# A vision tower on one core: the first logits moved ahead of the later embeddings, and the last results on another engine

## The reference, cut to what matters

```python
def reference(x, tok_W, tok_b, w1, b1, ww, bw, w2, b2, gamma, beta, w_gate, w_up, w_down):
    h = patchify(x) @ tok_W.T + tok_b                # 16 images x 64 patches, 768 -> 256
    v = h @ w1.T + b1
    w = softmax((v @ ww.T + bw).reshape(..., 16, 31))  # 16 heads, 31 taps; the axis of
    c = causal_conv(v, w)                            # time holds the 16 images
    a = layer_norm(h + (c @ w2.T + b2), gamma, beta)
    h = layernorm(h + a)
    g = silu(bitlinear(h, w_gate)) * bitlinear(h, w_up)
    return layernorm(h + bitlinear(g, w_down))
# bitlinear: the activations are rounded to 255 levels by each token's largest
# magnitude, the weights to -1, 0, 1 by the mean magnitude of the whole matrix
```

## Time and profile before

| | |
|---|---|
| median of 3 executions | 122.58 us |
| lowest, highest | 120.61, 123.64 us |
| the profiled execution: its own time | 121.21 us |
| its span in the profile | 119.4 us |
| busy in the span: PE, PEld | 102.3 (86%), 66.3 (55%) us |
| busy: DVE, ACT, POOL | 75.6 (63%), 71.6 (60%), 75.2 (63%) us |
| mean granted clock of TensorE | 0.976 |
| HBM read, written | 9.43, 2.34 MB |

### The profile page before, as it was taken

The page is one execution under the profiler, slowest core; times in us unless marked ns, Lnnn a source line. Parts: engine busy times, 40 slices in busy tenths (PEclk is TensorE's granted clock), DMA queues, the critical chain, the costliest instruction groups (busy, mean ns, idle before and its releaser), DMA issues. The chain is left out here.

```text
span 119.4 us, 2363 instructions
## 1 busy us (share of the span) xinstructions
PE 102.3 (86%) x714; PEld 66.3 (55%) x714; DVE 75.6 (63%) x184; ACT 71.6 (60%) x131; POOL 75.2 (63%) x147
## 2 busy tenths in 40 slices
PE   6938997399999999999999999999999997775400
PEld 2536885377677557755755666565665653354200
DVE  5229800004464574848798989889887889978710
ACT  0006121596686330477676798998688899879620
POOL 6995000000209596999656886888888988988840
PEclk9999999999999999999999999999999999999955
DMA  3999999910122132323233220232301010010232
GB/s 100 272 384 430 422 420 381 415 68 0 49 20 24 46 33 59 38 50 34 57 34 65 22 22 0 52 32 58 34 9 32 20 28 15 0 49 0 56 90 79
DMA packets 22099, 11.94 MB, mean 100 GB/s; under 512 B 17987, under 2 KB 20291, under 8 KB 21702
## 3 DMA queue, kind: packets, MB, share of 16 engines
q1 hardware_dynamic: 21436, 10.67, 31.7%
q10 hardware_dynamic: 650, 1.11, 2.6%
HBM read 9.43 MB, written 2.34 MB: 99 GB/s over the span
## 5 line engine op out<-in xcount | busy, mean ns | idle before, releaser
L1078 POOL TENSOR_TENSOR taps<-probs,inv_total 128x256 f32<-128x256 f32 x8 | 5.1, 635 | 20.4 <-DVE inv_total L792 20.1
L351 PE MATMUL bank<-xT,first 128*128 128x256 f32 x72 | 16.4, 380 | 0.3 <-ACT h1T L583 0.3
L429 PE MATMUL bank<-conv_w,vpad 128*32 128x128 f32 x256 | 15.9, 399 | 0.0
L771 DVE TENSOR_REDUCE top<-bank 128x16 f32<-128x496 f32 x8 | 5.3, 664 | 16.4 <-PE bank L412 16.3
L351 PEld LDWEIGHTS bank<-xT,first 128*128 128x128 f32 x72 | 13.5, 190 | 3.2 <-issue 0.9
L412 PE MATMUL bank<-ww,vT 128*128 128x496 f32 x32 | 14.6, 578 | 0.0
L667 ACT ACTIVATE gu<-bank,sc 128x512 f32<-128x512 f32 x16 | 11.0, 687 | 3.7 <-PE bank L486 3.2
L854 DVE TENSOR_TENSOR gu<-gu,bank 128x512 f32<-128x512 f32 x16 | 10.9, 683 | 2.6 <-ACT gu L667 2.6
L429 PEld LDWEIGHTS bank<-conv_w,vpad 128*32 128x32 f32 x256 | 8.6, 122 | 6.4 <-issue 3.1
L1104 POOL TENSOR_SCALAR q<-gu,sc 128x512 f16<-128x512 f32 x14 | 9.7, 694 | 2.6 <-DVE sc L871 1.5
L542 PE MATMUL bank<-w_q,q2T 128*128 128x256 f16 x64 | 9.0, 272 | 2.6 <-ACT q2T L681 2.2
(11 more groups left out here) (115 smaller groups left out, 228.4 us busy)
## 6 DMA issues: line engine op xcount, KB each, us to landing
xT<-in_xT SPq DMA_DIRECT2D x3, 768.0 KB, 14.9
first<-in_first SPq DMA_DIRECT2D x2, 512.0 KB, 6.5
w_raw<-in_wg SPq DMA_DIRECT2D x1, 1024.0 KB, 11.6
w_raw<-in_wu SPq DMA_DIRECT2D x1, 1024.0 KB, 13.8
w_raw<-in_wd SPq DMA_DIRECT2D x1, 1024.0 KB, 17.6
shear<-taps SPq DMA_DIRECT2D x8, 128.0 KB, 1.7
conv_w<-shear SPq DMA_DIRECT2D x64, 16.0 KB, 2.0
out_dram<-res SPq DMA_DIRECT2D x7, 128.0 KB
```

The lines of the kernel that those rows point to most:

```text
L351: last = nc.tensor.matmul(ps_embed(pair, m), tokW[:, k, m * P:(m + 1) * P], xT[:, pair - 1, k, :], start=(k == 0), stop=(k == KC_PATCH - 1))
L429: last = nc.tensor.matmul(ps_yT[j * SLOT:(j + 1) * SLOT, k, :], vpad[:, s, h, :], conv_w[:, s, :, h], start=(par == 0), stop=(par == 1))
```

## The change

The lists of TensorE and ScalarE are written anew for the first stage. On TensorE `logits(0)` comes ahead of `embed(1, 1)`, `logits(1)` ahead of `values_turned(1, 0)` and `embed(2, 0)`, `logits(2)` ahead of `embed(2, 1)` and `logits(3)` ahead of `embed(3, 0)`. On ScalarE `weight_sum(0)`, `(1)` and `(2)` are set apart, with copies and exponentials between them; `negate_gamma()` moves behind `weight_sum(2)`, and `weight_round(1)` behind `exps(3)`. In ScalarE's last tile `out_q1T(7)` comes ahead of `scaled_down(4)` and `silus(7, 1)` ahead of `out_q2T(5)`, and `result(3)` behind `out_q2T_last()`. The results of tiles 5, 6 and 7 are made by VectorE, `late_result(t)`, all behind `out_variance(7)`; GpSimd's `shift_result(5)` and `(6)` go; `f` has four buffers. SyncE stores tile 5 and the first half of tile 7, ScalarE tile 6 and the second half of tile 7.

```diff
+LATE = 5
-        f = sb("f", [P, 3, D])
+        f = sb("f", [P, 4, D])
-        last_ok = sem("last_ok")
+        late_ok = sem("late_ok")
+        def store_late(eng, t):
+            eng.wait_ge(late_ok, t - LATE + 1)
+            eng.dma_start(out_d[:, t * BLOCK:(t + 1) * BLOCK, :].rearrange("i b d -> b i d"),
+                          res[:, t % 4, :]).then_inc(out_done[t % 4], 16)
         def store_half(eng, j):
-            eng.wait_ge(last_ok, 1)
+            eng.wait_ge(late_ok, TILES - LATE)
# SyncE
-            store(0); store(1); store(2); store(3); store(4); store(5); store(6); store_half(sp, 0)
+            store(0); store(1); store(2); store(3); store(4); store_late(sp, 5); store_half(sp, 0)
# TensorE
-            first_embeds(); embed(1, 0); embed(1, 1); values_turned(0, 0); residual(0); values_turned(0, 1)
-            values_turned(1, 0); values(0); embed(2, 0); logits(0); embed(2, 1); logits(1); values_turned(1, 1)
-            values_turned(2, 0); values(1); values_turned(2, 1); weight_means(0, 2); logits(2); embed(3, 0)
-            weight_means(2, 3); logits(3); conv(0); logits(4); project_out(0); embed(3, 1); values(2); conv(1)
+            first_embeds(); embed(1, 0); values_turned(0, 0); values_turned(0, 1); residual(0); logits(0)
+            embed(1, 1); values(0); logits(1); values_turned(1, 0); embed(2, 0); values(1); values_turned(1, 1)
+            logits(2); weight_means(0, 2); embed(2, 1); values_turned(2, 0); logits(3); values_turned(2, 1)
+            weight_means(2, 3); embed(3, 0); conv(0); logits(4); project_out(0); embed(3, 1); values(2); conv(1)
# ScalarE
-            out_h1T(0, 0); out_h1T(0, 1); out_h1T(1, 0); out_h1T(1, 1); out_vT(0, 0); negate_gamma(); out_h1(0)
-            out_vT(0, 1); out_v(0); weight_sum(0); out_vT(1, 0); weight_sum(1); out_h1T(2, 0); exps(0)
-            weight_sum(2); out_h1T(2, 1); out_vT(1, 1); exps(1); out_v(1); out_vT(2, 0); out_vT(2, 1)
-            weight_round(1); out_h1T(3, 0); exps(2); exps(3); out_yT(0); out_v(2); exps(4); out_h1T(3, 1)
+            out_h1T(0, 0); out_h1T(0, 1); out_h1T(1, 0); out_vT(0, 0); out_vT(0, 1); out_h1(0); weight_sum(0)
+            exps(0); out_h1T(1, 1); out_v(0); weight_sum(1); out_vT(1, 0); exps(1); out_h1T(2, 0); out_v(1)
+            out_vT(1, 1); weight_sum(2); out_h1T(2, 1); negate_gamma(); exps(2); out_vT(2, 0); out_vT(2, 1)
+            exps(3); weight_round(1); out_h1T(3, 0); out_yT(0); out_v(2); exps(4); out_h1T(3, 1)
...
-            quant_in(7); scaled_down(4); out_q1T(7); result(2); silus(7, 0); out_q2T(5); silus(7, 1)
-            down_scale(5); down_scale(6); scaled_down(5); out_q2T(6); quant_last_half(); result(3)
-            scaled_down(6); out_q2T_last(); result(4); result(5); result(6)
-            store_half(act, 1)
+            quant_in(7); out_q1T(7); scaled_down(4); result(2); silus(7, 0); silus(7, 1); out_q2T(5)
+            down_scale(5); down_scale(6); scaled_down(5); out_q2T(6); quant_last_half()
+            scaled_down(6); out_q2T_last(); result(3); result(4)
+            store_late(act, 6); store_half(act, 1)
# scaled_down on ScalarE; down_result on VectorE waits likewise
-                if t >= 3:
-                    act.wait_ge(res_ok, t - 2)
+                if t >= 4:
+                    act.wait_ge(res_ok, t - 3)
# VectorE
-            def last_result():
-                dve.wait_ge(rstd_out, TILES)
-                dve.wait_ge(out_done[LAST % 4], 16)
-                nc.vector.tensor_scalar(res[:, LAST % 4, :], f[:, LAST % 3, :], mv[:, 2, LAST % 4, 0:1],
-                                        rstd[:, 2, LAST % 4, 0:1], ALU.subtract, ALU.mult).then_inc(last_ok, 1)
+            def late_result(t):
+                dve.wait_ge(rstd_out, t + 1)
+                dve.wait_ge(out_done[t % 4], 16)
+                nc.vector.tensor_scalar(res[:, t % 4, :], f[:, t % 4, :], mv[:, 2, t % 4, 0:1],
+                                        rstd[:, 2, t % 4, 0:1], ALU.subtract, ALU.mult).then_inc(late_ok, 1)
-            out_stats(7); out_variance(7); last_result()
+            out_stats(7); out_variance(7); late_result(5); late_result(6); late_result(7)
# GpSimd
-            inv_std_out(4); shift_result(4); add_centred(6); inv_std_out(5); shift_result(5); inv_std_out(6)
-            shift_result(6); inv_std_out(7)
+            inv_std_out(4); shift_result(4); add_centred(6); inv_std_out(5); inv_std_out(6)
+            inv_std_out(7)
```

More of the change, by code:

```diff
@@ L696, in result @@
                     act.wait_ge(out_done[t % 4], 16)
-                nc.scalar.activation(res[:, t % 4, :], f[:, t % 3, :], ACT.Identity, bias=shift_out[:, t % 4:t % 4 + 1],
+                nc.scalar.activation(res[:, t % 4, :], f[:, t % 4, :], ACT.Identity, bias=shift_out[:, t % 4:t % 4 + 1],
                                      scale=rstd[:, 2, t % 4, 0:1]).then_inc(res_ok, 1)
@@ L715, in scaled_down @@
                 act.wait_ge(down_scale_ok, t + 1)
-                if t >= 3:
-                    act.wait_ge(res_ok, t - 2)
-                nc.scalar.activation(f[:, t % 3, :], ps_down, ACT.Identity,
+                if t >= 4:
+                    act.wait_ge(res_ok, t - 3)
+                nc.scalar.activation(f[:, t % 4, :], ps_down, ACT.Identity,
                                      scale=sc[:, t % 4, 9:10]).then_inc(down_read, 1)
@@ L923, in down_result @@
                 dve.wait_ge(centred_ok, t + 1)
-                dve.wait_ge(res_ok, t - 2)
-                nc.vector.scalar_tensor_tensor(f[:, t % 3, :], ps_down, sc[:, t % 4, 9:10], centred[:, t % 6, :],
+                dve.wait_ge(res_ok, t - 3)
+                nc.vector.scalar_tensor_tensor(f[:, t % 4, :], ps_down, sc[:, t % 4, 9:10], centred[:, t % 6, :],
                                                ALU.mult, ALU.add).then_inc(down_read, 1)
@@ L933, in out_stats @@
                     dve.wait_ge(down_read, t + 1)
-                at["out", t] = mark(nc.vector.bn_stats(stats[:, 2, t % 2, :], f[:, t % 3, :]))
+                at["out", t] = mark(nc.vector.bn_stats(stats[:, 2, t % 2, :], f[:, t % 4, :]))
             def out_variance(t):
@@ L1110, in add_centred @@
                 pool.wait_ge(centred_ok, t + 1)
-                nc.gpsimd.tensor_tensor(f[:, t % 3, :], f[:, t % 3, :], centred[:, t % 6, :], ALU.add).then_inc(f_ok, 1)
+                nc.gpsimd.tensor_tensor(f[:, t % 4, :], f[:, t % 4, :], centred[:, t % 6, :], ALU.add).then_inc(f_ok, 1)
             def weight_round(j):
```

## The result

The changed kernel takes 123.82 us (median of 4, 123.48 to 124.51) where the kernel before, with its further run, takes 121.73 (median of 4). The ratio is 1.0237, with a 95% interval of 1.0179 to 1.0295: slower, while the interval leaves open whether by more or less than 2%. All ratios here leave out executions more than 1.5% above the fastest of their kernel, which takes out two of the four of the kernel before and makes this one larger than the ratio of the medians (1.017). The profiled executions are 121.21 and 123.48 us, 2.27 apart, their spans 119.4 and 121.6.

What follows compares the result with a forecast made beforehand. TensorE's queue from conv(0) to 97 us, then the end's chain to GpSimd, was taken as the bound. First stage +1.44 and end +0.26 gave +1.70, so 122.9 or 124.3 us by footing; 123.6 was taken, range 121.0 to 125.5.

Steps and rivals of the forecast that it cites:

- The six holes: First stage, TensorE: six open hand-offs sum to 4.30 us against one hole of 2.86, so conv(0) starts 1.44 later.
- the rigid shift: From conv(0) to 97 us: TensorE is full, so any shift of conv(0)'s start arrives at 97 us undiminished.
- the cover of weight_round(1): ScalarE, behind exps(3): the 2.10 us instruction delays out_yT(0) at no cost, with 0.9 us of cover before project_out(0).
- the weight chain: First stage: the first two weight means come earlier, but weight_means(2,3) at 39.4 as before, so nothing is gained.
- The silu order: End, ScalarE: silus(7,1) ahead of out_q2T(5) wins the silu 0.57 but makes down(5) and down(7) about 1.0 us later.
- the other edits: End: taking two shifts off GpSimd saves 0.65 us, and scaled_down(6) no longer behind result(3) another 0.1.
- the queue of GpSimd: End: without two shifts ahead, GpSimd takes up the last statistics as they come, saving 0.65 us.
- VectorE's results "hidden" in GpSimd's 0.93: End: VectorE makes results 5 and 6, 0.41 us each, within the 0.93 that GpSimd needs, at no cost.
- result(3) is done ahead of down_result(7): End: the moved result(3) finishes at 112.9, before down_result(7), which waits for it, at 113.2; cost 0.
- At this kernel's density a hole did not cost the clock: First stage: the granted clock was 1.00 behind the 2.86 us hole, taken as evidence against a clock loss.
- rival C: Early stage: the clock falls and one embed costs its 2.6 us again; +4.3, time 126.9, chance 0.05.
- The middle course between two footings: Whole time: 123.6 us, taken between 122.9 on the profiled execution and 124.3 on the median of three runs.

Runs made afterwards that it cites:

- e11: The changed kernel with weight_round(1) directly behind weight_sum(2) on ScalarE; 123.08 us, ratio 1.0274 to the kernel before.
- e4: The changed kernel with out_q2T(5) ahead of silus(7,1) again; 122.99 us, ratio 1.0118 to the kernel before.
- e1: The kernel before with only the new first-stage order on TensorE and ScalarE; 123.01 us, ratio 1.0157 to the kernel before.
- e6: The changed kernel with result(3) ahead of scaled_down(6) again; 123.21 us, ratio 1.0176 to the kernel before.
- e2: The changed kernel with the old first-stage order, all edits of the end kept; 122.92 us, ratio 1.0086 to the kernel before.
- e3: The kernel before with only negate_gamma() moved, behind out_h1T(2,1) on ScalarE; 118.73 us, ratio 0.9779 to the kernel before.
- e9: The changed kernel with the gamma and beta load issued late, by SyncE behind the last xT load; 123.31 us, ratio 1.0266 to the kernel before.
- e12: The changed kernel with logits(3) behind values_turned(2,1) and out_q2T(5) ahead of silus(7,1); 121.85 us, ratio 1.0101 to the kernel before.
- e7: The changed kernel with logits(3) behind values_turned(2,1) on TensorE; 124.71 us, ratio 1.0245 to the kernel before.
- e8: The kernel before with the gamma and beta load issued late, by SyncE behind the last xT load; 127.47 us, ratio 1.0612 to the kernel before.
- e5: The changed kernel with old first-stage order, negate_gamma() behind out_h1T(2,1), out_q2T(5) before silus(7,1), result(3) before scaled_down(6); 118.68 us, ratio 0.9830 to the kernel before.

## Why the prediction was right, and where it was not

**The early part.** Right in mechanism and place. The six holes, by the same starts as in the prediction, measure 0.60, 0.83, 0.68, 0.85, 0.84 and 0.68 (the second, for one: 22.57 - 21.49 - 0.25), 4.48 against 4.30 forecast. The term was +1.44 and F grew by 1.77. The holes were undersized by 0.18 in sum. Most of that is one restart: values_turned(1,1) starts 0.26 behind the end of ScalarE's copy (28.09 + 0.47 to 28.82) and not 0.14, where the other five restarts take 0.10 to 0.15. The rest is that a group which had waited reaches its copy 0.07 later (2.87 and 1.14 in place of 2.80 and 1.07). The remaining 0.15 of F is work that the prediction held to be the same, above all embed(3,0), which takes 2.76 to conv(0) where an embed took 2.59 to the next. I had taken the price of a restart from one row, of values(0).

**The stage behind it.** Right: full TensorE from conv(0) on, the rigid shift, the cover of weight_round(1) (e11), the weight chain where it was (VectorE reads the second mean at 39.99, before at 39.73).

**The end.** +0.26 was forecast, G shows +0.64. The silu order was right: priced at 1.01, it measures 1.09 at down(5) and 1.05 in G (e4). The gain that was set against it was too large: the other edits were priced at -0.75 and gain 0.41 (e4 against e1). Step by step, from e1 to the changed kernel: down(5) +1.09; from there to the last variance -0.13, priced -0.1; the queue of GpSimd -0.54, priced -0.65, as GpSimd still starts 0.10 behind the variance (115.75 + 0.18 = 115.93 to 116.03); and from there to the last result +0.22, priced at nothing. Together 0.64.

That last step is what failed: VectorE's results "hidden" in GpSimd's 0.93, and "result(3) is done ahead of down_result(7): 0". In e6, where no store is in the way, it is 1.01 from GpSimd's start to the last result, and GpSimd's first instruction of that root takes 0.34 in place of 0.27 while two results of VectorE run; it is 0.34 in all nine profiles with an edited end and 0.26 or 0.27 in the five with the old one:

```profile
115.23 0.34 POOL L1074 TENSOR_SCALAR veps<-veps,mv 128x1 f32<-128x1 f32 x1
```

The Trainium skill (SBUF — State Buffer, in its table of terms) has the two engines arbitrate for one pair of ports, the loser blocked while the other's instruction holds it. The longer row has the direction of that, but it is longer by 0.07 only, where one result of VectorE takes 0.41, and no run here isolates it. The other 0.15 is the store of tile 3 (e6). The step on result(3) looked at one reader only: the last result also waits for that store, which the move had put back.

On E alone the end would look as forecast, +0.29 from e1 to the changed kernel. That is luck: gate(7,1) came 0.35 earlier behind conv(0) in the one profile than in the other (63.17 and 63.52).

**The clock.** "At this kernel's density a hole did not cost the clock" is the sentence that fell. The row was right and the reading too wide: one profile had the clock at 1.00 behind the hole, that of e2 at 0.74. In the 55 executions of the kernel before beside the experiments, the 23 with a mean clock of 0.976 or more have a median of 120.72 us, the 32 below it one of 122.44. Of the kernels without the open hole, the changed one, e1, e3 to e6, e9, e11 and e12, none of 44 executions is under 0.976 (the low ones of e7 fall at its end, by its profile); of e2 and e8, which have it, nine of twelve are. Where in the kernel the clock fell is seen in the profiles of e2 and e8 alone; the kernel before has no profile of an execution with a low mean clock. The rival C on the other hand, a clock that falls for six short holes, did not come: 1.00 up to 98 us. The rule of the Trainium skill (TensorE: Matmul & The Clock Gate, "A second HAM failure mode: psum-queue depth-cycling") that I weighed for it did not show here: six idle times of 0.44 to 0.70 left the clock at 1.00. What the same page of the Trainium skill says in "Loop structure matters more than you think", that a long wait for a DMA ahead of the matmuls sends the clock down, is of the kind of e8, where TensorE idled 6.91 us for a copy that stood behind a DMA. In e2 the same wait was 2.33 us and the clock fell too, while the kernel before passed its 2.69 at 1.00.

**The number.** 123.6 was forecast and 123.82 measured, but the fair measure is the difference: +1.70 by the sum on the profiled execution, +2.27 measured there. The 0.57 between them is 0.33 in F and 0.38 in G, less what gate(7,1) came early, and some 0.1 behind the last result. The middle course between two footings happened to land close, and that is luck: 123.6 was put as 0.8% above the kernel before, whose median a further run moved from 122.58 to 121.73, and the measured 123.82 is 1.7% above that one; slower by over 2% had been given 0.24. I had guessed that late landings spread the runs of before; much of that spread is the clock, which also means that the kernel before loses by it what the changed one, without the long hole, does not.

## What to carry to other kernels

When a wait of another engine is found on the path, move the thing that waits, and nothing else, before any order is rewritten: one call gave 2.2% (1.7% by F and E), and with the new order around it the same move lost 1.6%. In an order written by hand, an instruction next to what it depends on costs the whole hand-off (copy, semaphore, restart: 0.6 to 0.85 us each here), which an independent matmul group between the two hides for nothing, as e7 and e12 show for one of the six. Price an edit from the last point that it cannot move, not from one far ahead of it: E blurred by 0.3 us what G shows to 0.02. And when a result is moved back in time, go through all its readers, the store behind it and whoever waits for that store too.

## What the runs showed that I had not expected

- The same hole of 2.3 to 2.9 us sometimes costs the clock and sometimes doesn't: an embed behind it took 2.76 (before) or 4.44 (e2), and 4.84 behind 6.91 us (e8).
- Filling such a hole with unread matmuls narrows eleven executions to 1.1 us.
- With a hole of 0.7 us closed early in the kernel (e7) the clock fell at 107 us in the profile, at a wait that the changed kernel had passed at 1.00, and three executions of four had such a low mean clock; 0.68 was gained in F and 2.83 lost in E. Why the earlier arrival should matter is open.
- The end's other edits shorten G by 0.41 (e4) and 0.60 (e5), and the medians don't show it.
